# Moving work between engines in an mLSTM-like layer with a quantised feed-forward block, on one core

## The reference

```
xn   = layernorm(x)                                  # over the 256 features
i,f,o,z = split(xn @ W + b)                          # W is 256 x 1024
i = 10*tanh((i + input_bias)/10);  f = -softplus(f);  o = sigmoid(o);  z = tanh(z)
m' = max(f + m, i);  i_s = exp(i - m');  f_s = exp(f + m - m')      # scan over the steps
c = f_s*c + i_s*z;   n = f_s*n + i_s;   h = o * c/(n + 1e-6)
x1 = x + scale * h / sqrt(mean(h^2) + 1e-8)
g  = layernorm(layernorm(x1)) * gamma + beta
w1 = (fc1_q - 128)*fc1_scales;  w2 = (fc2_q - 128)*fc2_scales       # int32 weights, groups of 128 rows
out = base + 0.5*(silu(g @ w1 + b1) @ w2 + b2),  base = x1 + layernorm(x1)
```

## Time and profile before

| | |
|---|---|
| median of 3 runs | 310.02 us (309.99 to 310.45) |
| the profiled execution | 311.77 us |
| its span, first to last instruction | 310.0 us |
| TensorE, VectorE, ScalarE, GpSimd busy | 95%, 87%, 74%, 41% of the span |
| mean granted TensorE clock | 0.988 |

### The profile page before, as it was taken

How to read it: one execution, slowest core, us unless ns; L and a number is a source line. 1 busy time by engine, 2 the same in 40 slices (tenths; PEclk the granted TensorE clock), 3 DMA queues, 4 the chain that set the end, 5 groups by cost and what they waited for, 6 DMA issues and landing times.

```text
span 310.0 us, 4767 instructions
## 1 busy us (share of the span) xinstructions
PE 294.7 (95%) x1728; PEld 256.3 (83%) x1728; DVE 269.5 (87%) x487; ACT 229.7 (74%) x370; POOL 126.4 (41%) x131
## 2 busy tenths in 40 slices
PE   7999999979899899999999999999999799988996
PEld 5778789856897789988897889987898699868896
DVE  3998989999899999999999997999999987692741
ACT  2699987889879966899876978599866983921720
POOL 3043058300290529512970179012992198155000
PEclk9999999899999999999999999999999979999999
DMA  7980021060000030012000300020000011000201
GB/s 266 349 304 0 0 44 27 0 135 2 0 1 2 34 101 5 0 66 71 1 2 34 102 2 0 0 71 1 0 2 34 3 33 68 2 0 2 70 0 68
DMA packets 11127, 14.73 MB, mean 48 GB/s; under 512 B 720, under 2 KB 10208, under 8 KB 10848
## 3 DMA queue, kind: packets, MB, share of 16 engines
q1 hardware_dynamic: 10368, 12.07, 11.3%
q0 software_dynamic: 320, 1.58, 2.6%
q10 hardware_dynamic: 416, 0.79, 0.7%
HBM read 8.67 MB, written 4.19 MB: 42 GB/s over the span
## 4 chain that ended last, share of the span: by engine, by line
PE 39%; DVE 38%; issue 11%; ACT 5%; POOL 5%; DMA 2%; DVEq 0%; POOLq 0%; ACTq 0%
PE z_ps L236 5%; PE z_ps L237 4%; PE z_ps L238 4%; DVE y_lo L854 4%; PE mm_ps L236 4%; PE mm_ps L237 4%; PE mm_ps L238 4%; DVE rec L763 3%; DVE rec L756 3%; DVE rec L778 3%; DVE g L822 3%; DVE bn L835 3%; PE mm_ps L329 2%; PE mm_ps L322 2%; DVE rows L830 2%
## 5 line engine op out<-in xcount | busy, mean ns | idle before, releaser
L236 PE MATMUL z_ps<-w_hi,y_hi 128*128 128x256 f32 x248 | 71.8, 290 | 2.6 <-DVE rows L891 1.9
L237 PE MATMUL z_ps<-w_lo,y_hi 128*128 128x256 f32 x248 | 70.9, 286 | 0.0
L238 PE MATMUL z_ps<-w_hi,y_lo 128*128 128x256 f32 x248 | 70.8, 286 | 0.0
L573 ACT ACTIVATE y<-mm_ps,b_all,unit 128x512 f32<-128x512 f32 x54 | 41.6, 770 | 12.8 <-PE mm_ps L329 12.8
L236 PEld LDWEIGHTS z_ps<-w_hi,y_hi 128*128 128x128 f32 x248 | 47.6, 192 | 3.8 <-DVE rows L891 2.1
L237 PEld LDWEIGHTS z_ps<-w_lo,y_hi 128*128 128x128 f32 x248 | 47.6, 192 | 0.3
L238 PEld LDWEIGHTS z_ps<-w_hi,y_lo 128*128 128x128 f32 x248 | 47.6, 192 | 0.0
L322 PE MATMUL mm_ps<-gt_hi,w_hi 128*128 128x512 f32 x124 | 39.9, 403 | 1.6 <-ACT y L573 1.6
L854 DVE TENSOR_TENSOR y_lo<-y,y_hi 128x512 fp32r<-128x512 f32 x56 | 37.6, 687 | 4.0 <-ACT y_hi L576 3.7
L236 PE MATMUL mm_ps<-xt_hi,wg_hi 128*128 128x512 f32 x96 | 38.4, 400 | 1.1 <-ACT f_gate L505 1.1
L329 PE MATMUL mm_ps<-gt_lo,w_hi 128*128 128x512 f32 x124 | 38.8, 394 | 0.0
(11 more groups left out here) (179 smaller groups left out, 665.2 us busy)
## 6 DMA issues: line engine op xcount, KB each, us to landing
out<-rows SPq DMA_DIRECT2D x15, 256.0 KB, 2.1
rows<-x SPq DMA_DIRECT2D x7, 512.0 KB, 6.5
q<-fc_q SPq DMA_DIRECT2D x2, 1024.0 KB, 10.8
wg_raw<-fc_scales SPq DMA_DIRECT2D x1, 1024.0 KB, 7.1
w_lo<-q POOLq DMA_DIRECT2D x1, 1024.0 KB, 7.0
wg_raw<-w_gates SPq DMA_DIRECT2D x1, 512.0 KB, 5.7
wg_raw<-w_gates ACTq DMA_DIRECT2D x1, 512.0 KB, 6.0
w_lo<-q POOLq DMA_DIRECT2D x1, 512.0 KB, 4.6
```

The source lines that it names most:

```text
L236: pe.matmul(dst, wh[w_at], ah[a_at], start=start, stop=False)
L237: pe.matmul(dst, wh[w_at], al[a_at], start=False, stop=False)
L238: return pe.matmul(dst, wl[w_at], ah[a_at], start=False, stop=stop)
L573: act.activation(y[:, j % YBUFS], fc1_bank(c, j), ACT.Silu, bias=b1_all[:, j:j + 1], scale=unit[:, j:j + 1]).then_inc(silu_done, 1)
```

## The change

The places where the order of the work or the engine changes:

- The scale vectors ratio and share are made on VectorE after chunk 1's x, no longer ahead of chunk 0's. Their two `spread` calls on TensorE move behind `x_turned(1)` and behind `h_turned(0)`. share is read from PSUM; its copy on ScalarE (2 activations) is gone. The rounding of w1 on ScalarE moves to chunk 2's gates.
- `base_bias` on VectorE is gone for all 8 chunks. GpSimd instead starts an accumulating transfer from b2_bc into rows behind each `base`; `final` waits for it.
- w2's low part is one subtraction on VectorE; the negation and the 1 MB transfer on GpSimd are gone. `fc2_first` does tiles n = 0 and 2 of chunk 0 with all low-part passes of w2 last.
- Chunk 3's gates are computed in the order i, z, f, o. Chunk 0's y_hi tiles 4 to 7 and chunk 6's 6 and 7 and chunk 7's odd ones are made by ScalarE, no longer by VectorE.
- Chunk 6's y_hi and y_lo lie in the weights of the gates, in xt and in a new buffer y_more. So `fc2(5,[3])` can run after `h_turned(7)`, and `fc2(6,[3])` after `fc1(7)`.
- `g_normalised(7)` moves from GpSimd to ScalarE. In chunks 5 to 7 GpSimd's base(5) is ahead of ln2_root(6), and both `final` calls of a chunk are moved forward on VectorE.
- VectorE's ln1_sums(4) and ln1_means(4) and GpSimd's ln1_root(4) come later.

```diff
@@ TensorE
             pe.wait_ge(ident_ready, 2)
-            pe.wait_ge(ratio_step, 2)
-            spread(ratio, z_bank).then_inc(ratio_spread, 1)
             for n in range(TT):
...
-            pe.wait_ge(share_ready, 1)
-            spread(share, lambda u: mm_ps[:, 2 + u]).then_inc(share_spread, 1)
-
             first_two_gates()
-            gates(0, range(2, 5))
+            gates(0, range(2, 6))
             x_turned(1)
-            gates(0, range(5, GJ))
+            pe.wait_ge(ratio_step, 2)
+            spread(ratio).then_inc(ratio_spread, 1)
+            gates(0, range(6, GJ))
...
             h_turned(0)
+            pe.wait_ge(gate_done, at(1, 8, 6))
+            pe.wait_ge(w1_scaled, 1)
+            pe.wait_ge(share_ready, 1)
+            spread(share).then_inc(share_spread, 1)
...
             gates(3, range(2, GJ))
-            fc2(0, range(0, 3))
+            fc2_first()
+            fc2(0, [1])
             g_turned(1)
-            fc2(0, range(3, TT))
+            fc2(0, [3])
             fc1(1, range(0, 2))
             x_turned(4)
-            fc1(1, range(2, 5))
+            fc1(1, range(2, 6))
             h_turned(2)
-            fc1(1, range(5, KF))
+            fc1(1, range(6, KF))
...
             fc1(5, range(KF))
-            fc2_both(5, 0)
+            fc2_both(5)
+            fc2(5, [1], range(0, KF // 2))
             g_turned(6)
-            fc2_both(5, 1)
-            fc1(6, range(0, 2))
+            fc2(5, [1], range(KF // 2, KF))
+            fc1(6, range(0, 5))
             h_turned(7)
-            fc1(6, range(2, KF))
-            fc2_both(6, 0)
+            fc1(6, range(5, 6))
+            fc2(5, [3])
+            fc1(6, range(6, KF))
+            fc2_both(6)
+            fc2(6, [1], range(0, KF // 2))
             g_turned(7)
-            fc2_both(6, 1)
+            fc2(6, [1], range(KF // 2, KF))
             fc1(7, range(KF))
+            fc2(6, [3])
             fc2(7, range(TT))
@@ TensorE, chunk 0's first tiles of fc2
+            def fc2_first():
+                first = [slice(n * P, n * P + P) for n in (0, 2)]
+                pe.wait_ge(silu_done, at(0, 8, 6))
+                pe.wait_ge(w2_rounded, 2)
+                for k in range(KF):
+                    pe.wait_ge(y_lo_done, k + 1)
+                    for u in range(2):
+                        pe.matmul(z_ps[:, u, 0], y_hi[:, k, first[u]], w2_hi[:, k], start=(k == 0), stop=False)
+                        pe.matmul(z_ps[:, u, 0], y_lo[:, k, first[u]], w2_hi[:, k], start=False, stop=False)
+                pe.wait_ge(w2_ready, 1)
+                for u in range(2):
+                    for k in range(KF):
+                        pe.matmul(z_ps[:, u, 0], y_hi[:, k, first[u]], w2_lo[:, k], start=False, stop=(k == KF - 1))
@@ ScalarE
-            silu(0, range(0, 4))
+            silu_alone(0, range(0, 2))
+            for j in range(2):
+                act.wait_ge(silu_done, at(0, 8, j + 1))
+                act.activation(y_hi[:, j], y[:, j], ACT.Copy).then_inc(y_hi_done, 1)
+            silu(0, range(2, 4))
             silu_alone(0, range(4, KF))
             square_sums(1)
+            gates(3, range(2, 4))
+            for j in range(4, KF):
+                act.wait_ge(silu_done, at(0, 8, j + 1))
+                act.activation(y_hi[:, j], y[:, j % YBUFS], ACT.Copy).then_inc(y_hi_done, 1)
             act.preload_act_table_set("sigmoid_and_others")
-            gates(3, range(2, GJ))
+            gates(3, range(4, GJ))
...
-            silu(1, range(2, 5))
+            silu(1, range(2, 6))
             square_sums(2)
-            silu(1, range(5, KF))
+            silu(1, range(6, KF))
@@ GpSimd, at the end of base(c)
+                pool.wait_ge(base_done, at(c, 4, 4))
+                pool.wait_ge(b2_halved, 1)
+                pool.dma_start(rows[:, b], b2_bc[:].unsqueeze(1).to_broadcast([P, TT, D]), accum_op=ALU.add
+                               ).then_inc(biased[c % 2], 16)
```

More of the change, by code:

```diff
@@ L330, in fc1, with fc2_block, fc2 @@
                     ins.then_inc(fc1_done, 1)
-            def fc2(c, tiles):
+            def fc2_block(c, n, k):
+                dst, rows_of = fc2_out(c, n), slice(n * P, n * P + P)
+                hi, lo = y_high_of(c, k)[:, rows_of], y_low_of(c, k)[:, rows_of]
+                pe.matmul(dst, hi, w2_hi[:, k], start=(k == 0), stop=False)
+                pe.matmul(dst, hi, w2_lo[:, k], start=False, stop=False)
+                return pe.matmul(dst, lo, w2_hi[:, k], start=False, stop=(k == KF - 1))
+            def fc2(c, tiles, blocks=range(KF)):
                 for n in tiles:
@@ L360, in fc2_both @@
-                        if half and k == KF - 1:
-                            ins.then_inc(fc2_done, 1)
+                        fc2_block(c, 2 * u, k)
             def x_turned(c):
@@ L1005, in _ @@
             x_low(4)
-            base_bias(0)
-            y_low(1, range(2, 3))
+            y_low(1, range(2, 4))
             mean_square(2)
-            y_low(1, range(3, 4))
             final(0, 0)
@@ L1033, in _ @@
                     x_low(t + 1)
-                    base_bias(t - 3)
-                    final(t - 3, 0)
                     y_low(t - 2, range(0, 1))
@@ L1051, in _ @@
                     h(t - 1)
-                    base_bias(t - 3)
+                    x_low(t + 1)
+                    input_times_z(t)
                     final(t - 3, 0)
-                    input_times_z(t)
-                    x_low(t + 1)
+                    final(t - 3, 1)
                     maximum(t, range(KD))
@@ L1078, in _ @@
             g_low(5)
-            base_bias(4)
             denominators(7, range(KD))
-            final(4, 0)
+            divisor(7)
             mean_square(6)
-            divisor(7)
             y_low(5, range(0, 1))
             h_scaled(6)
-            y_low(5, range(1, 2))
+            final(4, 0)
+            y_low(5, range(1, 3))
             residual(6)
-            y_low(5, range(2, 4))
+            final(4, 1)
+            y_low(5, range(3, 4))
             ln2_sums(6)
@@ L1095, in _ @@
             o_times_c(7)
+            g_low(6)
+            final(5, 0)
             newton(7)
             refined(7)
-            g_low(6)
             h(7)
-            base_bias(5)
-            final(5, 0)
-            final(5, 1)
             y_low(6, range(0, 2))
             mean_square(7)
-            y_low(6, range(2, 3))
             h_scaled(7)
+            final(5, 1)
             residual(7)
-            y_low(6, range(3, 4))
+            y_low(6, range(2, 4))
             ln2_sums(7)
@@ L1111, in _ @@
             ln2(7)
-            y_low(6, range(5, 6))
-            for j in range(6, KF):
-                y_high(6, j)
-                y_low(6, range(j, j + 1))
-            base_bias(6)
+            y_low(6, range(5, KF))
             g_low(7)
             final(6, 0)
+            y_low(7, range(KF))
             final(6, 1)
-            base_bias(7)
-            for j in range(KF):
-                y_split_last(j)
             final(7, 0)
```

199 lines of the change are left out of this document (89 added, 110 removed).

## The result

The changed kernel takes 305.83 us (median of 4 executions, 304.67 to 306.12) against 310.24 (309.99 to 311.15) for the kernel before on the same chip: a ratio of 0.985, 95% interval 0.982 to 0.988. It is faster. The forecast was 303.0 with a range of 300.3 to 307.5. The profiled span went from 310.0 to 302.9 us, 0.1 from the 303.0 of the sum; the medians moved by 4.4 us only, and `again` and the account of the median further down come back to that. Three executions ran slow at a mean clock of 0.753, 0.846 and 0.940, one of `again` (368.9 us) and the profiled ones of `z_late` (319.0) and `tail_finals` (306.8), and no time is compared with them.

A forecast was written before the change was run, and what follows sets the result against it. TensorE (294.7 of 310.0 us busy) was taken as the bound, gains coming only from its waits, VectorE second. 1.3 us up to 245 us plus 6.1 behind make 7.4, less 0.4 for handovers: 303.0 us, range 300.3 to 307.5.

The forecast's parts named there:

- Start, 0: Up to 65 us: 0.9 and 0.8 us gained, 1.7 lost to the two spreads between products, so nothing.
- 65 to 70 us, 1.6: With GpSimd's negation gone VectorE's copy is short; h_turned(1) starts near 68.7 instead of 70.31, 1.6 us ahead.
- 70 to 245 us: TensorE's lead goes up to 3.1 us, then 0.5, 1.7 and 0.55, and is 1.3 at the end.
- The y_lo wait: Near 82 us: TensorE newly waits 1.25 us for chunk 0's last y_lo, behind VectorE's subtraction for w2.
- I therefore give the remaining base_bias calls no value up to 245 us: VectorE's 1.34 us saved per chunk counted as nothing, since at t = 5 and 6 it then waits for x_high.
- The bound I had put on this choice, 1.2 us: If giving the removed bias additions no value up to 245 us was wrong, up to 1.2 us more gain.
- Behind 245 us, 6.1: From fc2_both(5)'s first matmul to the last end: 56.5 us against 62.6 before, so 6.1 us gained.
- The three parts: Stretches after fc2_both(5) starts: to h_turned(7) 15.4 us, on to g_turned(7) 15.1, to the end 26.0.
- g goes from GpSimd, 3.69 us, to ScalarE, -1.6: Between h_turned(7) and g_turned(7): normalising chunk 7's g takes 2.08 us on ScalarE, saving 1.6.
- The transfers, 0: Accumulating bias transfers take 4.6 to 5 us, bounds 2 and 10; cost 0 at 5 us.
- The rival: Bias lands late: 10 us transfers hold VectorE at finals of chunks 2 to 4; 310.7 to 313 us, chance 0.10.
- I keep that distance: The median stays 1.75 us below the profiled execution, as before: 304.8 profiled gives a median of 303.0.

The follow-up runs named there:

- again: The changed kernel itself, no edit, measured a second time: spans 302.6 to 302.9 us, median 304.52 us, ratio 0.980 to the kernel before.
- z_late: Changed kernel with chunk 3's f ahead of its z and ScalarE's table load ahead of its third tile: spans 302.7 to 302.9 us, median 304.59.
- tail_finals: As tail_old, but VectorE's two finals of chunk 4 and mean_square(6) in the changed order: span 305.1 to 305.2 us at a clock from 0.994.
- w2_pool: Changed kernel with w2's low part made as before, by GpSimd's negation and a transfer: span 303.3 to 304.2 us, median 305.63.
- iz_ahead: Changed kernel with VectorE's i*z moved ahead of x_low in turns 5 and 6: span 301.2 to 301.7 us at a clock from 0.994, median 303.41.
- bias_dve: Changed kernel with fc2's bias added by VectorE again, no bias transfers: span 306.8 to 307.1 us at a clock from 0.994, median 308.88.
- g7_pool: Changed kernel with g of chunk 7 normalised on GpSimd again: span 304.1 to 304.4 us, median 306.14.
- tail_old: Changed kernel with its last 60 us in the order of before, bias transfers kept: span 310.5 to 311.7 us, median 312.73.
- best: As iz_ahead, with h(2) and x_low(4) ahead of two y_low and chunk 2's squares one silu sooner: span 301.8 to 302.9 us, median 304.54.
- bias_tail_old: Changed kernel with the bias added by VectorE and the last 60 us in the order of before: span 310.1 to 313.4 us, median 314.0.
- iz_pool: Changed kernel with chunk 2's product i*z moved from VectorE to GpSimd: span 304.1 to 304.6 us.

## Why the prediction was right, and where it was not

**Start, 0: right.** The first gates start 0.9 sooner (10.00 for 10.94); by gates(2) at 40.09 it is level, 40.10 before.

**65 to 70 us, 1.6: right.** The copy takes 0.17, h_turned(1) is at 68.86 against 68.7 foretold, 1.45 ahead. w2_pool shows cause and size: the copy is 1.63 again and h_turned(1) 1.55 later.

**70 to 245 us: the end right, the way wrong.** The y_lo wait came, 0.8 by starts for 1.25, and the subtraction took 2.28, for which I had taken 2.3. But h_turned(2) was at 100.56 for 101.3 foretold and h_turned(3) at 131.51 for 132.45. At h_turned(2) TensorE was 1.25 ahead of before where I had 0.5, and w2_pool loses 1.24 there: the lead from 65 to 70 us is passed on nearly whole, which I had let the new waits use up. TensorE was 2.4 ahead at 242 where I had 1.3. It then waited for final(4,1) until 243.36, foretold 243.3, so the surplus was not cashed in: iz_ahead, in which the final is sooner, got 1.3 of it.

**The step that failed in mechanism: "I therefore give the remaining base_bias calls no value up to 245 us; they hold the place of the wait, no more."** True up to h_turned(4) (0.3 us in bias_dve), false from turn 6 on: 1.2 us at h_turned(5), 2.8 at h_turned(6), 4.2 at the end. The bound I had put on this choice, 1.2 us, was too small. The parts undone singly (4.2, 7.8, 1.1) add up to more than the whole change, so 4.2 is what the additions cost in the new order; what they cost in the old order no run shows. I had taken a wait of VectorE for room without following what it waited for back to VectorE.

**Behind 245 us, 6.1: right in its sum, and in one term by luck.** The three parts foretold as 15.4, 15.1 and 26.0 are 15.7 (243.36 to 259.08), 15.0 and 26.0. That counts from the end of the wait for final(4,1). Counted as before's 62.6 is, from fc2_both(5)'s first matmul (242.23), it is 57.85, a gain of 4.75, with 2.35 ahead of it: together 7.1 for the 7.4 of 1.3 + 6.1. The split was wrong by a little over 1 us and the sum held, because VectorE's final set the point 243.3 and TensorE's larger lead ended in a wait for it. The order of the finals carries this part. The term "g goes from GpSimd, 3.69 us, to ScalarE, -1.6" is worth 0: before, the 3.69 us from 276.04 on ran beside VectorE's last subtraction (276.25) and base_bias(6) (277.10); in g7_pool VectorE is idle there and GpSimd makes the four tiles in 2.17. What I gave to the move came from VectorE's place being empty.

**The transfers, 0: right as they are placed.** The rival needed a landing after 10 us; a final that follows the issue closely makes VectorE wait with 5.1 as well, 3.14 us in tail_old and 0.67 in `best`. The loss is smaller than the first of these waits, since tail_old's final(4,0) comes only 1.0 later than before and bias_tail_old is no faster without transfers.

**The median: the failed step is "I keep that distance".** The span was met, but I took 1.75 us off, the distance of before's profiled execution from its median. That execution had the clock's fall behind 245 us and 310.0 us; others had no fall anywhere and 307.4. Without any fall the change is worth 4.7 us (307.4 to 302.7), against the profiled execution of before 7.3, and by the medians of the second measurement 6.0. That the 7.0 of the sum met the profiled span rests in part on which execution of before was profiled. And the changed kernel's first median stood on executions with the long stretch, 1.4 us. Span plus 1.8 gives 304.7, which the profiled execution (304.67) and the second measurement (304.52) both have.

## What to carry over

Before calling an engine's wait room, follow what it waits for back through the other engines: when the path returns to the same engine, its work moves the wait and doesn't fill it. An asynchronous transfer is free only while its first reader stays far off, so look for that reader again with each new order (tail_old, `best`). When a part is undone singly, the result is its worth in the new kernel and not in the old one: both parts undone together gave neither the sum of the two nor the kernel before (bias_tail_old). Where half a per cent matters, sort executions by mean clock before comparing medians: one kernel's level changed by 1.4 us between two measurements.

## What the hardware showed that was not expected

- A GpSimd operation holds not only VectorE's copies (1.63 for 0.17 us) but a subtraction of two SBUF operands: 2.89 for 0.68 us beside a 2.78 us product. It goes the other way too, 3.69 us of GpSimd beside VectorE's two-input subtraction and addition, 2.17 where VectorE is idle. The Trainium skill (GPSIMD Engine Reference, "Specifications") says that GpSimd contends with VectorE instructions in a two-port mode or with two SBUF inputs; iz_pool's trace agrees, with 2.89 us for 0.68.
- The same instructions at 52 to 60 us ran with two lengths of 1.2 GHz. Told by a mean clock of 0.989, the long one came in 3 of 4 executions of the changed kernel in the first measurement, in none of 5 in the second and in 5 of 5 of g7_pool, the only one of these with a trace. What decides it stays open. The long one costs 1.4 us, the short one 0.
- An accumulating transfer of 512 KB from a broadcast source lands after 5.1 us (median of 8, the longest 6.2), against 4.6 for the single one with a plain source.
